# Selective scan: two VectorE operations of each item, one step later

## The reference, cut to what matters

```python
dt = softplus(dt_low_rank @ dt_proj.T + dt_bias)
def step(h, inp):
    x_t, dt_t, B_t, C_t = inp
    dA = exp(dt_t[..., None] * A)
    dBx = dt_t[..., None] * B_t[:, None, :] * x_t[..., None]
    h = dA * h + dBx
    y = einsum('bdn,bn->bd', h, C_t)
    return (h, y)
y = (ys + D_param[None, :, None] * xc) * silu(z)
out = einsum('bdl,hd->blh', y, out_proj_w)
```

## Time and profile before

| | us |
|---|---|
| median of 3 runs | 5375.42 (5373.48 to 5381.15) |
| the profiled execution, its own time | 5379.62 |
| its span in the profile | 5377.5 |
| the scan stage, first to last scan of it | about 2390 to 4272 of the span |

### The profile page before, as it was taken

The page is one execution under the profiler, slowest core; times in us unless marked ns, Lnnn a source line. Parts: engine busy times, 40 slices in busy tenths (PEclk is TensorE's granted clock), DMA queues, the critical chain, the costliest instruction groups (busy, mean ns, idle before and its releaser), DMA issues. The chain is left out here.

```text
span 5377.5 us, 50877 instructions
## 1 busy us (share of the span) xinstructions
PE 4828.1 (90%) x19376; PEld 2732.7 (51%) x19376; DVE 3124.8 (58%) x3354; ACT 2005.9 (37%) x2937; POOL 2171.3 (40%) x1187
## 2 busy tenths in 40 slices
PE   8998989999868899967788998999899899999998
PEld 4443234467536444435565665666566544457443
DVE  1673468756457322238888898888889622103522
ACT  1454520045322111136666566656666410002100
POOL 1003430000022000019998888999889642100421
PEclk9898999999989999989999999999999999999999
DMA  2001030000010122141116346434644420000001
GB/s 75 1 1 67 32 118 24 28 16 1 9 34 1 40 70 70 51 123 40 38 45 168 118 134 171 139 118 133 181 127 130 138 82 0 24 0 19 29 16 47
DMA packets 177488, 357.30 MB, mean 66 GB/s; under 512 B 21279, under 2 KB 56223, under 8 KB 173151
## 3 DMA queue, kind: packets, MB, share of 16 engines
q1 hardware_dynamic: 169182, 326.26, 20.0%
q0 software_dynamic: 8064, 27.80, 1.4%
HBM read 296.31 MB, written 57.67 MB: 66 GB/s over the span
## 5 line engine op out<-in xcount | busy, mean ns | idle before, releaser
L3018 POOL TENSOR_TENSOR l2scan_h<-l2scan_dtx,l2scan_Bb 128x1024 f32<-128x1024 f32 x384 | 902.0, 2363 | 73.0 <-PE l2scan_yT L2785 59.9
L2785 PE MATMUL l2scan_yT<-ident,l2scan_h 128*128 128x128 f32 x4096 | 551.5, 283 | 179.6 <-POOL l2scan_h L3043 169.6
L2785 PEld LDWEIGHTS l2scan_yT<-ident,l2scan_h 128*128 128x128 f32 x4096 | 484.9, 145 | 389.7 <-POOL l2scan_h L3043 238.3
L2968 ACT ACTIVATE l2scan_ring<-l2scan_dt,l2scan_A 128x512 f32<-128x512 f32 x768 | 508.4, 685 | 453.1 <-DVE l2scan_h L3101 243.7
L3043 POOL TENSOR_TENSOR l2scan_h<-l2scan_h,l2scan_Cb 128x1024 f32<-128x1024 f32 x256 | 604.0, 2359 | 44.8 <-DVE l2scan_h L3090 34.5
L2767 PE MATMUL l2scan_big<-state,l2scan_Wz 128*128 128x512 f32 x1024 | 472.9, 594 | 0.4 <-ACT l2scan_zs L2923 0.4
L2411 PE MATMUL l2in_acc<-state,l2in_W 128*128 128x512 f32 x1024 | 445.0, 595 | 10.5 <-DMA l2in_W<-l_attn_in_x 10.5
L2536 PE MATMUL l2scan_big<-l2scan_oy,l2scan_oW 128*128 128x512 f32 x768 | 362.9, 603 | 12.3 <-DMA l2scan_oy<-l_y 12.0
L2411 PEld LDWEIGHTS l2in_acc<-state,l2in_W 128*128 128x128 f32 x1024 | 194.4, 190 | 258.7 <-issue 247.4
L3101 DVE TENSOR_TENSOR l2scan_h<-l2scan_ring,l2scan_Cb 128x1024 f32<-128x1024 f32 (+1 forms) x307 | 315.5, 1042 | 4.4
L3090 DVE TENSOR_TENSOR_SCAN l2scan_ring<-l2scan_ring,l2scan_carry,l2scan_h 128x512 f32<-128x512 f32 x256 | 313.0, 1268 | 7.8 <-ACT l2scan_ring L2968 7.8
(11 more groups left out here) (426 smaller groups left out, 8497.5 us busy)
## 6 DMA issues: line engine op xcount, KB each, us to landing
l2scan_oy<-l_y SPq DMA_DIRECT2D x192, 512.0 KB, 5.2
l2scan_Wz<-l_attn_in_z SPq DMA_DIRECT2D x64, 512.0 KB, 3.5
l2scan_oW<-l_attn_out_w SPq DMA_DIRECT2D x192, 128.0 KB, 3.5
l_xc<-l2in_xc SPq DMA_DIRECT2D x16, 1024.0 KB, 4.8
l2scan_xc<-l_xc SPq DMA_DIRECT2D x64, 256.0 KB, 4.8
l2scan_Cb<-l_bc SPq DMA_DIRECT2D x128, 128.0 KB, 6.7
l_y<-l2scan_zs SPq DMA_DIRECT2D x64, 256.0 KB, 3.7
l2scan_Bb<-l_bc SPq DMA_DIRECT2D x96, 128.0 KB, 5.8
```

The lines of the kernel that those rows point to most:

```text
L2785: last = t.matmul(yT[:, k, :], h[:, st % SLOTS, j, k * P:(k + 1) * P], K.ident[:, :], is_transpose=True, start=g == 0 and j == 0 and k == ...
L2968: a.activation(bank(st, j) if maker(st) == "P" else h[:, st % SLOTS, j, :], dt[:, q % 2, :], ACT.Exp, scale=A[:, ct, n:n + 1]).then_inc(dA ...
L3018: g_.tensor_tensor(h[:, st % SLOTS], dtx[:, None, :].to_broadcast([P, SGR, NT]), Bb[:, rows_at(g), :], ALU.mult).then_inc(dBx_ok, 1)
```

## The change

VectorE's `pre_c` of the next item is taken up behind step 4 of the item (index g = 4, the fifth step) and no longer behind step 3. It now stands directly ahead of `pre_dt`. The addition of an output tile, `proj.add`, is taken up behind step 5 (the sixth step) and no longer behind step 4. Nothing is added or removed.

```diff
@@ -3102,11 +3102,11 @@
                     if g == 6 and q:
                         finish(q - 1)
-                    if g == 3 and q + 1 < ITEMS:
+                    if g == 4 and q + 1 < ITEMS:
                         pre_c(q + 1)
                     if g == 4 and q + 1 < ITEMS:
                         pre_dt(q + 1)
-                    if g == 4 and q >= CT and q % 2 == 1:
+                    if g == 5 and q >= CT and q % 2 == 1:
                         proj.add(v, (q - CT) // 2)
```

## The result

The changed kernel took 5354.61 us (median of 7 runs, 5336.08 to 5358.98) beside 5373.68 for the kernel before (7 runs, 5371.10 to 5389.90): ratio 0.9955, interval 0.9940 to 0.9969. A second measurement (e7), beside runs of the kernel before with a median of 5380.79, gave 5350.34, ratio 0.9942, interval 0.9926 to 0.9959. By the ratios it is faster by 24 and 31 us, by the medians by 19 and 30; my sum was 21.7, my forecast 5353. The profiled execution of the changed kernel has a span of 5352.5 us.

What follows compares the result with a forecast made beforehand. A closed loop of waits through DVE, POOL and PE over each pair of items was taken to bound the scan stage. Gains of 6.5, 4.6, 6.6 and 4.0 us, together 21.7, from 5375.42 gave 5353 us, range 5334 to 5366.

Steps and rivals of the forecast that it cites:

- my sum: Predicted gain over chunks 0 to 3: 6.5, 4.6, 6.6 and 4.0 us, together 21.7 us.
- The loop: Scan stage, per pair of items: mark to L3060 26.56, to POOL's dtx 0.76, POOL's product 12.98, PE's stretch 16.92; 57.22 us.
- Only the even item's wait counts: Of L3055's two waits for ACT in a pair, only the even item's was said to be on the closed loop.
- L3060 1.22 earlier: DVE, even item: L3060 was to start at 4054.19 instead of 4055.41, the wait at L3055 less 0.05.
- my bound: Spacing from L3055's start to L3060's directly behind it: at least 0.61, at most 0.80 us; 0.73 taken.
- The addition costs 0.60 a pair in chunks 1 and 3: The output tile's addition, now behind step 5's scans on DVE, puts 0.60 us on the loop there; hidden in chunk 2.
- the mark: Start of DVE's scans of step 5 in the odd item, from which a pair is counted.
- What is late next: POOL's `low` limits L3060 in chunks 0 and 2, with gains of 0.92 and 0.83 a pair; not in chunks 1 and 3.
- 1 (all waits back): Rival: all of L3055's waits come back, in odd items too; 5292 us, chance 0.04.
- 2 (the addition hides): Rival: addition hides or `low` is less late, chunks 1 to 3 keep the whole even wait; 5344 or 5337 us, chance 0.10.
- 3 (nothing but chunk 0's 6.5 us, a ratio of 0.9988): Rival: gain stays in chunk 0, DMA waits or PE take up the rest in chunks 1 to 3; 5369 us, chance 0.12.
- 4 (slower): Rival: even items' L3060 waits for `low` at its old time, the addition costs 0.6 in 24 pairs; 5390 us, chance 0.06.

Runs made afterwards that it cites:

- e7: The changed kernel measured a second time, unchanged; 5350.34 us, ratio 0.9942 to the kernel before.
- e4: Kernel before with the correction moved after step 4 in odd items only, the addition as before; 5381.72 us, ratio 1.0006.
- e1: Kernel before with only the correction moved after step 4, the addition left after step 4 as before; 5342.57 us, ratio 0.9928.
- e3: Kernel before with the correction moved after step 4 in even items only, the addition as before; 5336.49 us, ratio 0.9922.
- e11: The kernel of e1 measured again; 5341.33 us, ratio 0.9927.
- e2: Kernel before with only the output tile's addition moved after step 5, the correction left after step 3; 5383.49 us, ratio 1.0006.
- e10: As e1, but in even items the correction and the sum for dt stand ahead of step 4's product; 5334.76 us, ratio 0.9917.
- e12: As e10, but in odd items the correction stands in step 3, as in the kernel before; 5331.59 us, ratio 0.9912.
- e6: Changed kernel with half of the output projection's matmuls left out, their loads kept; 5316.68 us, ratio 0.9880 to the kernel before.
- e9: Changed kernel with half of the output projection's matmuls and their loads left out; 5268.68 us, ratio 0.9798 to the kernel before.
- e8: Kernel before with half of the output projection's matmuls and their loads left out; 5307.04 us, ratio 0.9860.

## Why the prediction was right, and where its sizes were off

**The loop: right.** All four members are there, the three behind L3060 with 0.77, 12.99 and 17.08 against 0.76, 12.98 and 16.92. What was taken off another place changed nothing that can be told (e4); what was taken off the loop changed the time (e1, e3).

**Only the even item's wait counts: right**, by e3 and e4.

**L3060 1.22 earlier: 1.11** (the sum counted 1.17). Two sizes: the usual wait of an even item was 1.20 and not 1.27, and L3060 starts 0.79 after L3055 (4088.02 to 4088.81) where I had taken 0.73. It starts 0.10 after L3055's end, at the upper end of my bound. I had called that 0.10 the time in which ACT and POOL take up DVE's results; the rows of POOL show 0.08 (4056.09 to 4056.17). The Trainium skill, "VectorE: DVE Perf Modes", section "The DRAIN you can't avoid", has a semaphore behind a VectorE operation cost nothing extra, which would have put it at 0.61, the spacing without a wait; the trace says 0.79, so waiting for the neighbour's result costs 0.18 here. In the 15 even items of chunks 1 and 3, where it is on the path, that is 2.7 us.

**The addition costs 0.60 a pair in chunks 1 and 3: right** from the mark to L3060 (25.98 against 25.38 in e1). In chunk 2 it is hidden, as predicted: 25.61 with it and without it. e1 is 8 to 12 us faster than the changed kernel by the medians; 15 pairs by 0.60 are 9, though over whole pairs the traces show 0.4.

**What is late next: right in place.** In chunk 0, L3060 of the changed kernel stands directly behind `low`'s end, 2584.41 + 1.27 = 2585.68:

```profile
2585.72 0.69 DVE L3060 TENSOR_TENSOR l2scan_dt<-l2scan_l,l2scan_small 128x512 f32<-128x512 f32 x1 [0.79 <-POOL l2scan_l L2998]
...
2584.41 1.27 POOL L2998 TENSOR_TENSOR l2scan_l<-l2scan_l,l2scan_dt 128x512 f32<-128x512 f32 x1
```

The gain was 0.81 a pair and not 0.92, because I had read the one item of chunk 0 that was out of line. In it L3060 started 0.97 behind `low`'s end; in the six other even items behind the chunk's first it was 0.83 to 0.86, as in this one of the kernel before (DVE, then POOL):

```profile
2645.59 0.68 DVE L3060 TENSOR_TENSOR l2scan_dt<-l2scan_l,l2scan_small 128x512 f32<-128x512 f32 x1
...
2643.47 1.26 POOL L2998 TENSOR_TENSOR l2scan_l<-l2scan_l,l2scan_dt 128x512 f32<-128x512 f32 x1
```

In chunk 2 the even item waits 0.36 for `low` (0.3 predicted); first three rows DVE, the last POOL:

```profile
3388.97 0.69 DVE L3055 SCALAR_TENSOR_TENSOR l2scan_small<-l2scan_small,l2scan_u 128x512 f32<-128x512 f32 x1
3390.02 0.69 DVE L3060 TENSOR_TENSOR l2scan_dt<-l2scan_l,l2scan_small 128x512 f32<-128x512 f32 x1 [0.36 <-POOL l2scan_l L2998]
...
3412.44 2.35 DVE L3090 TENSOR_TENSOR_SCAN l2scan_ring<-l2scan_ring,l2scan_h 128x512 f32<-128x512 f32 x2 [1.35 <-ACT l2scan_ring L2968]
...
3388.71 1.28 POOL L2998 TENSOR_TENSOR l2scan_l<-l2scan_l,l2scan_dt 128x512 f32<-128x512 f32 x1
```

From the mark to L3060 the gain there is 26.44 - 25.61 = 0.83, as predicted. The whole pair gained 0.67 on the median (58.15 to 57.48) and 0.58 on the mean, because the other part of the loop was longer: the PE stretch of chunk 2 took 17.49 on the mean against 17.18, of which 0.18 are waits for loads (0.42 against 0.24). In e7, a second execution of the changed kernel, it took 17.17, and the seven pairs of chunk 2 gained 0.84 each on the mean (58.08 to 57.24), as predicted; in e1 and e11 it took 17.19 and 17.08. So the shortfall belongs to one execution, not to the change, and a good half of it was the landing of loads. A new wait came up that I had not foreseen: in odd items of chunk 2 the scans of step 4 wait up to 1.35 for ACT's exponentials (row 3412.44). It isn't on the loop, since L3060 waits another 2.61 for `low` behind it.

**What I missed: the clock of PE.** The sum of chunks 1 and 3 was 8.6 us; their measured pairs, seven of each, give 13.6 (405.67 to 398.80 and 408.63 to 401.88). For chunks 0 and 2 the sum had 13.1, and the same traces give 5.7 and 4.0, that is 9.7 (the sum counts eight pairs in chunks 1 and 2, the traces seven). That the total came so near is in part luck: one part was too small and the other too large. The steady part of the 13.6 is 14 pairs by 0.51, 7.1 us. The rest is in the kernel before, in four stretches where PE's clock fell. The busy time and the granted clock of two PE stretches of the kernel before, one disturbed and the one of the prediction's pair, and of two single microseconds at the head of the disturbed one:

```profile
core 0: us, PE busy (x) PEld busy (x) DVE busy (x) ACT busy (x) POOL busy (x), PEclk, DMA share, GB/s
3061.83:3080.64 18.81, 18.49 (x76) 11.38 (x77) 13.44 (x14) 10.75 (x18) 15.23 (x8) 0.92 0.42 145
4069.16:4086.07 16.91, 16.86 (x76) 10.26 (x77) 13.38 (x13) 10.70 (x18) 14.87 (x8) 1.00 0.50 162
3062.00:3063.00 1.00, 1.00 (x6) 1.00 (x7) 1.00 (x2) 0.10 (x1) 1.00 (x1) 0.50 1.06 406
3065.00:3066.00 1.00, 1.00 (x3) 0.38 (x2) 1.00 (x1) 0.67 (x2) 1.00 (x1) 0.99 0.00 0
```

and PE there:

```profile
3058.88 0.60 PE L2807 MATMUL l2scan_small<-ident,l2scan_dtx 128*128 128x128 f32 x4
3061.88 1.97 PE L2785 MATMUL l2scan_yT<-ident,l2scan_h 128*128 128x128 f32 x8 [2.40 <-POOL l2scan_h L3043]
3063.64 4.29 PE L2536 MATMUL l2scan_big<-l2scan_oy,l2scan_oW 128*128 128x512 f32 x8
```

The eight matmuls of L2785 take 1.97 and not 1.09, at a granted clock of 0.50 (that is 1.2 of 2.4 GHz), and the stretch 18.8 and not 16.9. Ahead of it PE stood idle for 2.40 us. In the traces of the three full kernels whose even item's correction stands in step 3 (before, e2, e4) PE has that wait of 2.4 in all but two of the pairs counted (the first of chunk 1 in e2 and e4 has 0.8), and the clock falls in 4, 3 and 4 of 13 stretches, each time behind a wait of 2.4. In the seven with the correction behind or ahead of step 4's product (after, e7, e1, e3, e10, e11, e12) the wait is 1.8 or less and it falls in none of 91. In chunk 2, behind waits of 2.3 to 2.6, it falls in 0, 3 and 2 of 7 stretches of before, e2 and e4, and with 1.5 in the other seven kernels in none. From L3060 to the mark the four disturbed pairs take 32.84 on the mean and the nine others 31.08, so each costs 1.8 us and the four 7.0; with the steady 7.1 that is 14.1 against the 13.6 measured. So no step of the loop failed but its constancy: I had read one undisturbed pair and taken it for all, although the kernel before had pairs of 59.05 to 59.62 in chunks 1 and 3. That the shorter idle time is what keeps the clock up is an association over the traces, not shown: no run changed PE's idle time alone. The nearest are e6 and e9. Their correction stands behind step 4's product, as in the changed kernel, but PE has less to do and waits 3.25 in e6 and mostly 2.4 to 2.8 in e9, and the clock falls in 9 and 7 of 13. That speaks for PE's idle time and load, and against the place of the correction as such. The stage's mean of 0.97 before and after hides all this, since chunk 0 alone has a mean clock of 0.94 and 0.93 in the two kernels.

**The rivals.** 1 (all waits back) fell by e4. 2 (the addition hides) fell by the 0.60 between e1 and the changed kernel in chunks 1 and 3; their totals alone say it less surely, as the intervals of the ratios touch. 3 (nothing but chunk 0's 6.5 us, a ratio of 0.9988) fell with the ratio. 4 (slower) needed a `low` that is late in chunks 1 and 3; it ends 4086.90 + 1.27 = 4088.17, 0.64 ahead of L3060.

## What to carry to other kernels

Where several engines are each 85 to 90% busy, walk one period of the schedule and list which waits are on the closed loop: here half of one engine's 105 us of waits was worth the whole gain and the other half nothing that can be told, and one operation of 0.6 us put behind the loop's mark cost 0.6 us of that part of the loop in each period (0.4 over the whole period) although the engine had idle time elsewhere. Walk several periods, not one, and compare the granted clock of those that are longer. A move that takes work off the loop and another that puts work on it should be tried apart: the correction alone gave 36 and 40 us by the medians (e1, e11), both together 19 and 30. And ask what a wait waits for: in e2 the addition did not vanish in a wait of 1.2 us, because the awaited result came later too.

## What the runs showed of the hardware

- PE's granted clock fell to 0.50 (for about 3 us in the one shown) behind an idle time of 2.4 us in 11 of 37 stretches of chunks 1 and 3, behind 3.2 to 3.3 us in e8 (where PE also had less work) in 13 of 13, behind 1.6 to 3.0 us in e9 (the same) in 7 of 13, and behind 1.8 us or less in the seven full kernels with the correction in step 4 in none of 91. The turns of the chunks are not counted.
- DVE's L3060 starts 0.10 us after the end of L3055 directly ahead, whose result it needs (4088.02 + 0.69 to 4088.81); L3101 starts 0.03 after the scans that it needs. Without such a need an operation starts 0.08 before the end of the one ahead, so the need costs 0.11 to 0.18 us on these 128x512 tiles.
- Leaving out half of PE's matmuls of the projection but not their loads turned 50 us of PE's time into waits for those loads (10.9 to 61.0).
